# A Mamba block with a mixture of experts on one core: out-projection, delta projection, softplus steps and top-two in another order

## What is computed

```python
sa, ca, ga, sb, cb, gb = six modulation rows per batch
h = layernorm(x) * (1 + ca) + sa
x, z = split(h @ in_proj_w.T)               # 256 channels each
x_bld = silu(conv(x) + conv_b)
dt, Bm, Cm = split(x_bld @ x_proj_w.T)      # 8, 16, 16
delta = softplus(dt @ dt_w.T + dt_b)
A = -exp(A_log)                             # 256 x 16
h_t = h_{t-1} * exp(delta_t * A) + (delta_t * x_bld_t) * B_t    # a scan over 512 steps
y_t = sum over the 16 states of h_t * C_t
y = (y + x_bld * D) * silu(z)
x = x + ga * (y @ out_proj_w.T)
h = layernorm(x) * (1 + cb) + sb
# experts: softmax router, top 2 of 8, exact gelu, one shared expert
weights = router probabilities of the two best experts, else 0
x = x + gb * (shared(h) + sum over e of expert_e(h) * weights_e)
```

## Time and profile before

| | us |
|---|---|
| median of 3 runs | 786.83 |
| lowest and highest run | 786.34 and 788.0 |
| the profiled execution | 784.51 |
| its span from first to last instruction | 782.7 |

### The profile page before, as it was taken

The page is one execution under the profiler, slowest core; times in us unless marked ns, Lnnn a source line. Parts: engine busy times, 40 slices in busy tenths (PEclk is TensorE's granted clock), DMA queues, the critical chain, the costliest instruction groups (busy, mean ns, idle before and its releaser), DMA issues.

```text
span 782.7 us, 9866 instructions
## 1 busy us (share of the span) xinstructions
PE 622.5 (80%) x3454; PEld 475.3 (61%) x3454; DVE 619.5 (79%) x733; ACT 429.9 (55%) x637; POOL 322.6 (41%) x172
## 2 busy tenths in 40 slices
PE   6565477898969996997969996999879856996597
PEld 4223344777456954776457953777557745695377
DVE  4198997979977998979697997979996998597302
ACT  2579434893368634884278534884479314810260
POOL 1025554435543554434353654534542545344000
PEclk9878569799869998899979997899979966997599
DMA  6403243132431333222431242222422332300000
GB/s 193 181 38 130 114 162 124 55 108 108 152 108 54 108 135 124 80 83 111 152 108 54 108 148 111 86 77 108 155 90 76 140 135 108 121 1 14 0 1 14
DMA packets 26372, 77.83 MB, mean 99 GB/s; under 512 B 2817, under 2 KB 17234, under 8 KB 18130
## 3 DMA queue, kind: packets, MB, share of 16 engines
q1 hardware_dynamic: 25842, 76.75, 27.2%
q10 hardware_dynamic: 480, 0.43, 0.2%
HBM read 74.55 MB, written 2.62 MB: 99 GB/s over the span
## 4 chain that ended last, share of the span: by engine, by line
PE 48%; DVE 25%; ACT 11%; issue 11%; POOL 3%; DMA 1%; ACTq 0%; DVEq 0%; POOLq 0%
DVE state L1054 12%; PE psum L506 8%; PE psum L479 7%; PE psum L628 5%; DVE psum L1045 4%; PE psum L596 4%; PE psum L598 3%; PE psum L597 3%; PE psum L553 3%; POOL state L405 3%; ACT h L883 2%; PE psum L532 2%; ACT decay L765 2%; PE psum L524 2%; PE psum L575 2%
## 5 line engine op out<-in xcount | busy, mean ns | idle before, releaser
L405 POOL TENSOR_TENSOR state<-state,bc 128x1024 f32<-128x1024 f32 x128 | 302.3, 2362 | 372.6 <-DVE psum L1045 372.2
L1054 DVE TENSOR_TENSOR_SCAN state<-decay,psum 128x1024 f32<-128x1024 f32 x128 | 291.7, 2279 | 9.4 <-PE psum L479 2.0
L479 PE MATMUL psum<-ident,state 128*128 128x128 f32 x1024 | 152.3, 299 | 41.9 <-POOL state L405 41.9
L765 ACT ACTIVATE decay<-delta,a_neg 128x511 f32<-128x511 f32 x256 | 162.9, 709 | 28.4 <-DVE state L1054 28.3
L479 PEld LDWEIGHTS psum<-ident,state 128*128 128x128 f32 x1024 | 132.1, 156 | 57.8 <-POOL state L405 50.9
L1045 DVE TENSOR_TENSOR psum<-bc,du 128x1024 f32<-128x1024 f32 x128 | 157.5, 1231 | 4.6 <-DVE state L1054 0.6
L628 PE MATMUL psum<-down_w,h 128*128 128x128 f32 x1024 | 127.2, 278 | 6.3 <-DVE gT_mix L1153 6.3
L628 PEld LDWEIGHTS psum<-down_w,h 128*128 128x128 f32 x1024 | 119.1, 192 | 15.9 <-DVE gT_mix L1153 9.4
L883 ACT ACTIVATE h<-psum,vec 128x512 f32<-128x512 f32 x144 | 96.8, 688 | 13.7 <-PE psum L598 12.5
L506 PE MATMUL psum<-h_sb,conv_in_wT 128*128 128x512 f32 x128 | 65.3, 661 | 18.0 <-ACT h_sb L775 15.4
L1153 DVE TENSOR_TENSOR gT_mix<-psum,w 128x512 f32<-128x512 f32 x64 | 42.6, 684 | 35.9 <-PE psum L628 26.7
(11 more groups left out here) (134 smaller groups left out, 615.3 us busy)
## 6 DMA issues: line engine op xcount, KB each, us to landing
bc<-bc_rows SPq DMA_DIRECT2D x64, 1024.0 KB, 4.7
x_sb<-_attn_hidden_states_dram SPq DMA_DIRECT2D x9, 256.0 KB, 2.8
out_dram<-out_sb SPq DMA_DIRECT2D x8, 256.0 KB, 2.4
x<-_attn_hidden_states_dram SPq DMA_DIRECT2D x7, 256.0 KB, 3.0
h<-in_L_ffn_rw_dram SPq DMA_DIRECT2D x1, 1024.0 KB
bc_rows<-rows SPq DMA_DIRECT2D x8, 64.0 KB, 2.6
h<-in_L_wmod_dram ACTq DMA_DIRECT2D x1, 384.0 KB
h<-in_L_attn_in_proj_w_dram SPq DMA_DIRECT2D x1, 256.0 KB, 4.6
```

The source lines that it names most:

```text
L405: pool.tensor_tensor(state[:, u % STATE_RING, :, :], state[:, u % STATE_RING, :, :], bc[:, pair % BC_RING, 1, first:first + NU, :], ALU.mu ...
L479: last = nc.tensor.matmul(Y[q][:, t * P:(t + 1) * P], state[:, u % STATE_RING, s, t * P:(t + 1) * P], ident[:, :], start=False, stop=(u in ...
L765: last = nc.scalar.activation(decay[:, r, s, 1:L], delta[:, b.p, q, 1:L], ACT.Exp, scale=a_neg[:, q, k:k + 1])
L1054: nc.vector.tensor_tensor_scan(state[:, u % STATE_RING, :, :].rearrange("p n t -> p (n t)"), decay[:, u % DECAY_RING, :, :].rearrange("p n ...
```

## The change

Three engines get another order; no instruction is added or taken away, and no operand, buffer or wait changes.

```diff
 TensorE, slots(b, a, n, m)
                     g_transpose(a, n)
+                if b:
+                    y_start(b)
+                if a:
+                    out_proj(a)
                 if n:
                     dt_proj(n)
                 if a:
-                    out_proj(a)
-                if b:
-                    y_start(b)
+                    att_transpose(a)
+                if b:
                     y_add(b, 0)
-                if a:
-                    att_transpose(a)
-                if b:
                     y_add(b, 1)
                 if a:
                     x1_transpose(a)
-                    router(a)
                 if b:
                     y_add(b, 2)
                 for k in range(M_UP):
                     if a:
                         up(a, n, k)
+                        if k == 0:
+                            router(a)
 ScalarE, slots(b, a, n, m)
                     g_rows(a, n)
+                if a:
+                    att_rows(a)
                 if n:
                     softplus_relu(n)
-                if a:
-                    att_rows(a)
-                if n:
                     softplus_abs(n, a)
                     softplus_exp(n)
 VectorE, slots(b, a, n, m)
                     split_h2(a)
+                if b:
+                    scan_input(b, 5)
+                if a:
                     logits(a)
                 if b:
-                    scan_input(b, 5)
                     scan(b, 5)
-                if a:
-                    top2(a)
-                if b:
                     scan_input(b, 6)
                 if m:
                     stats(m)
                 if b:
                     scan(b, 6)
+                if a:
+                    top2(a)
                 if m:
                     xhat(m)
                 if b:
                     scan_input(b, 7)
                     scan(b, 7)
-                if n:
+                if n and not b:
                     make_delta(n)
...
                 for u in range(8, UN):
...
                     if b:
                         scan(b, u)
+                    if n and b and u == 9:
+                        make_delta(n)
```

More of the change, by code:

```diff
@@ L669, in slots @@
                 if a:
-                    out_proj(a)
-                if b:
-                    y_start(b)
-                    y_add(b, 0)
-                if a:
                     att_transpose(a)
                 if b:
+                    y_add(b, 0)
                     y_add(b, 1)
@@ L894, in slots @@
                     g_rows(a, n)
-                if n:
-                    softplus_relu(n)
                 if a:
@@ L899, in slots @@
                 if n:
+                    softplus_relu(n)
                     softplus_abs(n, a)
@@ L1218, in slots @@
                     scan(b, 7)
-                if n:
+                if n and not b:
                     make_delta(n)
-                    if isinstance(n.i, int) and n.i == 0:
-                        split_up_weights()
+                if n and isinstance(n.i, int) and n.i == 0:
+                    split_up_weights()
                 for u in range(8, UN):
```

## The result

| | before | after |
|---|---|---|
| median, us | 786.59 | 824.53 |
| lowest and highest of 4 runs | 784.54 to 788.0 | 820.06 to 824.86 |
| the profiled execution | 784.51 | 824.86 |
| its span | 782.7 | 823.1 |
| mean granted clock | 0.877 | 0.853 |

A forecast was written before the change was run, and what follows sets the result against it. DVE was taken to bound the kernel, full from the first `mix_block` to slot end, the expert chain nearly as tight. 33.3 - 2.2 + 8.4 + 3.95 + 2.15 = 45.6 us on 784.5 makes 830.1; forecast 830, range 808 to 846.

The forecast's parts named there:

- 1, delta: `make_delta` behind unit 9: the logarithm wait goes, but 4.43 us land in DVE's full stretch; 2.76 us lost per slot.
- 2, router late: Router behind `up(0)` on TensorE: its result, and with it the first gelu and `down(0)`, come 2.75 us later.
- 3, wait at `logits`: DVE, with `scan_input(5)` put ahead of `logits`, waits 2.2 us for the router's result, where there was 0.62.
- 3, wait at `mix_block(0)`: DVE reaches the slot's first `mix_block` early and waits 8.5 us for `down(0)`.
- 4, out-projection: Out-projection ahead on TensorE: shorter residual waits, net 0.5 to 0.9 us where DVE waited, 2.2 us off in all.
- 5, gap and clock: TensorE idles 2.7 us before the first gelu, its clock falls: 1.4 us lost per slot, bounds 0 and 3.
- six slots: The steady slots: 5.55 us lost in each, plus 1.4 each for the clock, minus 2.2 in all for the out-projection.
- slot without n: `mix_block(0)` already waited for `down(0)`, so the chain's shift is paid in full: 2.75 + 1.4, less 0.2: 3.95 us.
- last slot: `up(0)` and router end at about 742.75 us instead of 740.6: 2.15 us lost.
- the clock is up at the router: Rival: TensorE at 2.4 GHz there, router's shift 1.3 us instead of 2.75, nothing falls; 807 us, chance 0.09.
- My upper bound, 10.5: Most the out-projection's move could gain, in us, were every DVE wait at the residual to vanish.
- second fall behind delta: Rival: TensorE runs dry some 3.5 us while DVE makes delta, clock falls again, up to 2.5 us per slot; 845, chance 0.13.

## Why the prediction was right, step by step

| step | predicted | shown |
|---|---|---|
| 1, delta | 16.6 | 14.8 alone, 16.7 in the changed kernel |
| 2, router late | 2.75 later | 2.62 later |
| 3, wait at `logits` | 2.2 | 2.10 in four slots, 0.70 in two |
| 3, wait at `mix_block(0)` | 8.5, with step 5 9.9 | 9.2 to 11.5 |
| 4, out-projection | -2.2 | all 10.5 us of waits but 0.2 |
| 5, gap and clock | 2.7, 1.4 per slot | 2.8 in five slots, 5.19 in two; 1.37 |
| ahead of the first of these slots | 0 | 0.66 |
| six slots | 39.5 | 32.8 |
| slot without n | 3.95 | 3.98 |
| last slot | 2.15 | 2.94 |
| sum | 45.6 | 40.4 |

**Steps 1 and 2 held.** Delta stands in a stretch where DVE has no idle time, and its wait was worth less than its work. The router's end, measured from `split_h2`, is 2.62 us later; the router's row is 1.71 instead of 1.88. ACT is idle 2.82 us ahead of the router's exponential in this slot, where I had 2.9. The prediction had for the router's eight passes an estimate of 0.85 us, by the Trainium skill's rule for a weight load ("TensorE: Matmul & The Clock Gate", section "LDWEIGHTS (loading the stationary operand)"). The trace comes near it only at the higher clock: 0.95 us in the two slots of the changed kernel in which the clock was up at the router, 1.71 in the others.

**Step 3 held in its numbers and missed a mechanism.** In the four steady slots where DVE waited 2.1 us for the router, the readout was over before L1108 needed the ports, and L1108 took 0.19. In the two where the clock was up, the router came 1.4 us sooner, within the readout, and L1108 was stretched (one of them):

```profile
234.89 0.19 DVE L1102 TENSOR_TENSOR gT_mix<-psum,router_bias 128x32 f32<-128x32 f32 x1 [0.69 <-PE psum L575]
235.33 1.37 DVE L1108 TENSOR_TENSOR gT_mix<-gT_mix,router_stats 128x32 f32<-128x32 f32 x1
```

0.69 + 1.37 is about 2.10 + 0.19, and these slots last 91.07 and 90.90 us like the others. The late router and the stretched instruction delay one and the same chain: either alone costs about 30 us (31.5 and 30.1), both together, with `logits` behind, 824.5 - 788.5 = 36. My sum came out right because I had the one that is last; that the other, unseen cost lay under it was luck. It also means that my rival "the clock is up at the router", 807, could not have come true for its reason: two slots met its condition, and their first gelu stands at 25.4 us from the slot's start instead of 25.6.

**Step 4 was mis-sized; it is the step that failed.** I had 2.2 us for it: the `y_add` taken off PE's path less the copy laid bare, net 0.5 to 0.9 us, in slots whose waits I took as fixed. The runs show 13 us for it alone, and the waits of 10.5 us gone but for 0.2 in the changed kernel. Runs showed that the waits depend on something else: out-projections at 1.2 GHz in some slots. With `y_start` ahead, they ran at 2.4 GHz in the steady slots and the waits vanished. Why the clock stays up there is open. 6 x (5.55 + 1.4) = 41.7, less the 8.8 us of the three waits in the six slots (3.48, 1.84, 3.47), is 32.9; measured 32.8. My upper bound, 10.5, was the right value in the profiled execution. The sign of it was in the trace: 3.78 and 1.98 us for the same four matmuls in two slots. I had looked at one slot, and that was one without the wait.

By the medians the sum closes too, with errors that partly cancel: out-projection -13.3, delta +14.8, router and `logits` +36 make 37.5, measured 37.9. In the prediction these parts are -2.4, +16.6 and +31.4 (the last from steps 2, 3 and 5). So, as far as the intervals allow, the late chain cost some 5 us more than I had, and that hid a part of the 11 us missing in step 4. The out-projection's and delta's parts have intervals of 4 to 5 us either way.

**Step 5 held in its price; what the clock did is another matter.** The gap is there ([2.77 <-ACT h L884] above). The first gelus of the changed kernel:

```profile
426.56 1.83 ACT L884 ACTIVATE h<-psum,vec 128x512 f32<-128x512 f32 x3
428.97 0.69 ACT L884 ACTIVATE h<-psum,vec 128x512 f32<-128x512 f32 x1 [0.58 <-PE psum L598]
```

From the first gelu to `down`'s first row it is 445.62 - 426.56 = 19.06 us, before 426.86 - 409.17 = 17.69: 1.37 more. But in five of the seven slots the clock did not fall in the gap. It was low already, as before, and came up later: in this slot it is 0.50 from 414 us to 430, 3 us past the gap, where before it was 0.50 from 399 to 409 and up by the time of the first gelu. Only in the two slots with the clock up at the router did it fall, in a gap of 5.19 us. Filling the gap gave back 12.5 us, 9.8 expected. Where the surplus comes from wasn't taken apart.

**The rival "second fall behind delta"** happened and cost next to nothing. PE idled 3.54 us, the granted clock from 461 to 465 us is 0.57, and the `down` behind it took 3.68 instead of some 2.0 us (row at 460.94), but the `mix_block` behind waited only 0.16 us: DVE was the slower one there. I had priced PE's loss as if DVE waited for all of it.

**The last slot** was 0.8 us off. DVE waited 0.46 us longer for the residual (8.92 for 8.46), 2.0 longer for the router (3.25 for 1.24) and 0.5 longer for `down(0)` (17.59 for 17.08), which is about 3.0 for 2.94 measured. I had counted the router's part alone.

**The noise.** I had said that 0.2%, 1.6 us, could be told from no change. The kernel before scatters by almost 10 us, and the intervals of the experiments are 0.3 to 0.7% wide to each side.

## What to carry to other kernels

An instruction moved out of a wait must land where its engine is idle. If the wait stands ahead of full work, it is better to move other work into the wait (-22 us alone, here) than the waiting work away (+15). And when an instruction changes places with another, ask what the other one releases: here a multiply released a GpSimd operation that shut out the very instruction put behind it. A slot read in detail is one slot; a short look at the same row in all slots tells which costs are fixed and which come from the clock.

## What the runs showed of the hardware

- A VectorE instruction of 128x32 elements with both inputs in SBUF takes 0.19 us alone and 2.15 us when it starts 0.3 us behind a GpSimd multiply of 2.37 us; a reduction with one input, within the same multiply, keeps its 0.19. In the chain to the gelus this cost 25 us of 816, over seven slots.
- TensorE's clock level at the same program place differs from slot to slot of a periodic program (3.78 or 1.98 us for the same matmuls), and eight transposes of 1.04 us moved ahead put it at 2.4 GHz in all six steady slots: 13 us for a change that adds no work. Moving a scan on VectorE did the same. Why is open.
- The granted clock can fall while TensorE is busy: from 1.00 to 0.51 at 211 us, 1.7 us after 1.51 us of idle time; in other slots the same idle time was followed by no fall.
- More work can be faster: two unused matmuls per slot, in gaps of 2.8 us and more, took 12.5 us off.
